# The first layer's shared expert: the last 64 of its 704 rows as one step for two token groups

## Chip, cores and metric

The kernel runs on one core of a Trainium2 chip. The metric is the device time of one execution in microseconds (us). PE is TensorE, DVE is VectorE, ACT is ScalarE, POOL is GpSimd, SP is SyncE, which issues DMAs.

## The reference, cut to what matters

Two layers, each with a state-space branch and a mixture of experts on the same layer-normed input of 2048 tokens by 256. In the first layer the experts' part has a shared expert that all tokens pass through:

```python
x = hidden_states.reshape(-1, H)                # 2048 tokens, H = 256, float32
combine = ...                                   # top 4 of 16 experts, from x @ gate_w.T
shared = _silu_mul(x @ shared_gate_up.T, SI) @ shared_down.T      # SI = 704
shared = shared * jax.nn.sigmoid(x @ shared_gate_vec.T)
# _silu_mul(gu, inter) = silu(gu[:, :inter]) * gu[:, inter:]
```

Beside it stand the routed experts (inner size 176), a selective scan over 16 states (which needs projections of x to 64 rows for delta and to 32 rows for B and C), and the second layer, which is not touched.

## The kernel before, in words

Each engine has one instruction stream, written out by hand, and semaphores order the streams against each other. Phase 0 stands between the layer norm and the first layer's loop over routed experts and scan. It does the whole shared expert, and lays the router's work and the scan's projections between its steps.

The tokens are in four groups c of 512 (NB = 4). The 704 inner rows are in six tiles f (F0 = 6): five of 128 rows and one of 64, padded with zero columns to 128. A **step** n = 6c + f, one of 24, is the "up" of one tile for one group:

- PE (`shared_up_tensor`, L699): for gate and up weights, two matmuls each over the contraction of 256, into two of the banks 0 to 3, by turns of n. It waits on `sh_free` until DVE has done step n - 2. Every float32 matmul stands as two records in the trace, so a step has 8.
- ACT (`shared_tanh`, L720): tanh of the gate's bank.
- DVE (`shared_silu`, L727 and L729): two passes that end in the slot n % 8 of the hidden activations `shT0`, which lie in the memory of the tile `y`.

When the six tiles of a group are there, the **downs** come (`shared_down_tensor`, L711): for each of the group's four blocks j of 128 tokens, six matmuls (12 records) accumulate over f into bank 4 or 5, by turns, and DVE adds the bank to x (`shared_add`, L741). A down waits on `sh_pfree` until the add two before it is done. `downs_at(n)` puts the downs of group c behind step 6c + 7, that is 7, 13 and 19; those of group 3 stand at the end of the phase, between DVE's work on delta (L961, L963).

Between the steps, by tables of the step's number:

- `SIDE_UP` and `SIDE_DOWN` place 16 **side products**. 0 to 3 are the 64-row projections (L807), 4 to 7 those for B and C (L812), 8 to 15 the products for delta (L817, contraction of 64). All use bank 7 and wait on `side_free` until the one before it has been read. For 8 to 15, ACT takes Abs and Exp (L828, L830) and DVE four passes (L853, L854, L856, L859), of which the first frees the bank and the last counts `z_free`. ACT's Ln at the end (L910) waits for all eight.
- The router: DVE builds the token lists at steps 0 to 13 (the long ones: L409 to L435 at step 7, L441 at steps 8 to 10, L449 at 11 and 12, L458 at 13), PE's 64 small matmuls that need them (L312, `route_tokens_tensor`) stand behind step 14, and DVE's last part behind step 15.

In `pads0_vector` DVE sets the padding of the weights to zero.

## Time and profile before

| | us |
|---|---|
| median of 3 runs | 1198.66 |
| lowest and highest of them | 1188.22, 1200.18 |
| the profiled execution | 1190.8 |
| its span, from the first to the last instruction | 1189.0 |
| its mean granted TensorE clock | 0.945 of full speed |

The profile is of one execution, so durations and waits are read from it and compared with its own 1190.8 us; the median of the runs is 7.9 us above it. In a timeline row the first number is the start from the span's start and the second the length in us; "[5.63 <-DVE x L741]" is the idle time of the engine before the row, and what ended it. A line such as L711 is one of the kernel before.

### The profile page before, as it was taken

What the parts mean: (1) busy time and instruction counts of PE and PEld (TensorE: products, weight loads), DVE (VectorE), ACT (ScalarE), POOL (GpSimd) and SP (SyncE); (2) the same over time, 40 slices, a digit from 0 to 9 for tenths busy, and PEclk for the clock granted to TensorE, in tenths of its full rate; (3) what the DMA queues carried; (4) which work ended last, traced back from release to release, by engine and by line L of the source; (5) the groups of instructions that cost most, each with busy time, mean ns of one, the idle gap of its engine ahead of it and who ended that gap; (6) DMA issues with size and microseconds to landing.
All of it is one profiled execution on the core that took longest, in us unless ns stands there. A gap on an engine that the chain in (4) does not pass through costs nothing.

```text
span 1189.0 us, 18608 instructions
## 1 busy us (share of the span) xinstructions
PE 970.0 (82%) x6048; PEld 573.3 (48%) x6048; DVE 902.7 (76%) x1508; ACT 495.4 (42%) x1130; POOL 413.9 (35%) x331
## 2 busy tenths in 40 slices
PE   3988998777787787774598867889988989899895
PEld 2354554444444444441545533545555655456553
DVE  4669567999999999999557644776677767777686
ACT  2201135555555555553032134544545554454542
POOL 2000010688877877763200011222322232132310
PEclk9989899999999999996899878989998999899997
DMA  6960081688878888888840042333433343244524
GB/s 217 371 187 1 12 207 47 146 155 159 161 144 163 157 157 160 139 162 169 205 140 5 1 108 54 90 95 87 112 90 94 89 109 93 68 101 101 115 43 142
DMA packets 108657, 144.30 MB, mean 121 GB/s; under 512 B 30789, under 2 KB 98899, under 8 KB 104275
## 3 DMA queue, kind: packets, MB, share of 16 engines
q0 software_dynamic: 30368, 77.92, 33.1%
q1 hardware_dynamic: 78195, 65.18, 19.8%
q8 instruction: 52, 0.85, 0.3%
q14 instruction: 42, 0.34, 0.1%
HBM read 73.72 MB, written 39.58 MB: 95 GB/s over the span
## 4 chain that ended last, share of the span: by engine, by line
PE 45%; DVE 22%; DMA 10%; issue 8%; ACT 6%; POOL 6%; SPq 2%; ACTq 1%; DVEq 0%; POOLq 0%
PE bank L699 7%; DMA sum<-yo,to_i 6%; PE bank L1902 6%; PE bank L1446 4%; PE bank L711 4%; POOL sum L1178 3%; PE bank L1452 3%; POOL xg L1185 3%; DVE cv L2159 2%; PE bank L1941 2%; PE bank L1024 2%; DVE xnT L1159 2%; PE bank L1885 2%; PE bank L1041 2%; PE bank L1894 2%
## 5 line engine op out<-in xcount | busy, mean ns | idle before, releaser
L1517 POOL DMA_INDIRECT sum<-yo,to_i x48 | 78.0, 1625 | 320.3 <-ACT yo L1475 297.9
L1185 POOL DMA_INDIRECT xg<-xn_d,token_i x80 | 95.9, 1198 | 175.7 <-DVE to_i L473 94.0
L1178 POOL DMA_INDIRECT sum<-yo,to_i x80 | 139.8, 1748 | 46.0 <-issue 21.3
L1024 PE MATMUL bank<-areaA,xgT 128*128 x320 | 116.2, 486 | 15.6 <-issue 8.7
L1041 PE MATMUL bank<-areaA,hidT 88*128 x320 | 90.7, 406 | 46.8 <-ACT hidT L1089 43.3
L2104 DVE TENSOR_TENSOR areaD<-areaD,gb 128x512 f32<-128x512 f32 x128 | 87.4, 688 | 50.6 <-ACT areaD L2051 49.6
L1902 PE MATMUL bank<-xnT,w_in 128*128 128x512 f32 x160 | 86.7, 668 | 6.6 <-ACT cv L2017 5.4
L1041 PEld LDWEIGHTS bank<-areaA,hidT 88*128 88x128 f32 x320 | 54.9, 190 | 76.4 <-issue 72.1
L1507 POOL DMA_INDIRECT xg<-xn_d,token_i x48 | 54.4, 1133 | 104.4 <-DVE to_i L473 90.0
L699 PE MATMUL bank<-xnT,areaB 128*128 128x512 f32 x192 | 86.8, 599 | 0.8 <-DVE y L729 0.8
L1024 PEld LDWEIGHTS bank<-areaA,xgT 128*128 128x128 f32 x320 | 55.0, 191 | 59.4 <-issue 42.7
L2051 ACT ACTIVATE areaD<-bank 128x512 f32<-128x512 f32 x128 | 75.8, 592 | 16.1 <-PE bank L1894 14.7
L1446 PE MATMUL bank<-wst,xgT 128*128 128x352 f32 x192 | 72.3, 501 | 5.9 <-ACT xgT L1462 3.5
L1071 ACT ACTIVATE areaB<-delta,a_neg 128x1022 f32<-128x1022 f32 x64 | 72.8, 1137 | 4.2 <-DVE areaB L1159 4.2
L2159 DVE SCALAR_TENSOR_TENSOR cv<-xpad,conv_w,cv 128x512 f32<-128x512 f32 x72 | 54.0, 750 | 15.1 <-ACT cv L2017 13.4
L720 ACT ACTIVATE areaB<-bank 128x512 f32<-128x512 f32 x24 | 14.3, 597 | 122.6 <-PE bank L699 122.6
L1096 ACT ACTIVATE yo<-bank,slot_w 128x256 f32<-128x256 f32 x80 | 37.6, 471 | 57.8 <-PE bank L1041 57.0
L994 PE MATMUL bank<-parts,pick 96*128 96x512 bf16 x128 | 40.6, 400 | 22.4 <-DVE xnT L1159 11.0
L699 PEld LDWEIGHTS bank<-xnT,areaB 128*128 128x128 f32 x192 | 35.4, 190 | 48.4 <-issue 44.4
L1941 PE MATMUL bank<-areaD,xq 128*32 128x64 f32 x2048 | 56.1, 230 | 2.9 <-DVE areaD L2112 2.9
L711 PE MATMUL bank<-areaB,y 128*128 128x256 f32 x192 | 48.8, 416 | 11.2 <-DVE x L741 11.2
L1941 PEld LDWEIGHTS bank<-areaD,xq 128*32 128x32 f32 x2048 | 35.6, 112 | 44.9 <-issue 35.2
(340 smaller groups left out, 2104.9 us busy)
## 6 DMA issues: line engine op xcount, KB each, us to landing
y<-xnT POOLq DMA_DIRECT2D x21, 1024.0 KB
wst<-gu_f SPq DMA_DIRECT2D x96, 176.0 KB
y<-areaB POOLq DMA_DIRECT2D x11, 1024.0 KB
wst<-down_f SPq DMA_DIRECT2D x48, 176.0 KB
areaA<-in_gu SPq DMA_DIRECT2D x2, 2816.0 KB
gu_f<-in_gu POOLq DMA_DIRECT2D x1, 5632.0 KB, 18.5
sum<-yo SPq DMA_DIRECT2D x2, 2176.0 KB, 16.1
down_f<-in_down POOLq DMA_DIRECT2D x1, 2816.0 KB, 24.5
```

Of the source, the lines that this page charges most:

```text
L699: last = nc.tensor.matmul(bank[:, b, :], w[:, k, f * P:(f + 1) * P], xnT[:, k, c * 512:(c + 1) * 512], start=(k == 0), stop=(k == KD - 1))
L711: last = nc.tensor.matmul(bank[:, 4 + n % 2, 0:D], shT[:, (c * F + f) % shT.shape[1], j * P:(j + 1) * P], sd[:, f, :], start=(f == 0), sto ...
L1024: last = nc.tensor.matmul(bank[:, GB + q % 2, 0:2 * FI], xgT[:, q % 2, k, :], wgu0_of(e, k), start=(k == 0), stop=(k == KD - 1))
L1041: last = nc.tensor.matmul(bank[:, HY, 0:D], hidT[:, q % 2, h, :], wd0_of(e, h), start=(h == 0), stop=(h == 1))
L1178: nc.gpsimd.indirect_dma_start(sum0_d[q % 2], bass.IndirectOffsetOnAxis(ap=to_i[:, q:q + 1], axis=0), yo[:, q % 5, :], None, compute_op=AL ...
L1185: nc.gpsimd.indirect_dma_start(xg[:, q % 5, :], None, xn_d[0], bass.IndirectOffsetOnAxis(ap=token_i[:, q:q + 1], axis=0)).then_inc(s.gathe ...
L1446: last = nc.tensor.matmul(bank[:, eb, 0:2 * FI], xgT[:, q % 2, k, :], wgu_of(q, k), start=(k == 0), stop=(k == KD - 1))
L1517: nc.gpsimd.indirect_dma_start(sum1_d, bass.IndirectOffsetOnAxis(ap=to_i[:, q:q + 1], axis=0), yo[:, q % 4, :], None, compute_op=ALU.add). ...
L1902: last = nc.tensor.matmul(o, w_in[:, k, col:col + P], xnT[:, k, b * L:(b + 1) * L], start=(k == 0), stop=(k == KD - 1))
L1941: last = nc.tensor.matmul(bank[32 * c:32 * c + 32, YB, at_t:at_t + Q], window, mm[:, g, j * Q:(j + 1) * Q], start=(old % 2 == 0 and g == 0 ...
L2104: nc.vector.tensor_tensor(mm[:, g, :].rearrange("p (j t) -> p j t", t=Q), ex[:, g % 2, :].rearrange("p (j t) -> p j t", t=Q), gb[:, step % ...
L2159: last = nc.vector.scalar_tensor_tensor(cv[:, m % 2, :], xpad[:, m % 2, i:i + L], conv_w[:, j, i:i + 1], cv[:, m % 2, :], ALU.mult, ALU.add)
```

## The change

The steps become 22. For each pair of groups (0 and 1, then 2 and 3) the 64 rows of tile 5 come first, as one step for both groups: the first group's result goes to rows 0 to 63 of the bank, the second's to rows 64 to 127, each by matmuls of 64 weight columns. Then come the five full tiles of the first group and those of the second. The table `UP_ROWS` lists the steps and `UP_SLOT` the slot of `shT0` that each writes. In a down the last matmul contracts over 64 rows only, rows 0 to 63 or 64 to 127 of the shared slot, and the 64 weight rows of `sd0` are loaded twice, once for either half. The zero padding goes.

The tables of side products and the router's step numbers are the same, so they now meet other steps: a group's last up is step 5, 10, 16 and 21, and its downs stand behind steps 7, 12 and 18 and at the end.

```diff
+        UP_ROWS = [(c, f) for p in range(NB // 2) for c, f in
+                   [(2 * p, F0 - 1)] + [(2 * p + h, f) for h in range(2) for f in range(F0 - 1)]]
+        UP_SLOT = (7, 0, 1, 2, 3, 4, 5, 6, 0, 1, 2, 3, 4, 5, 6, 0, 1, 2, 7, 4, 5, 6)
+        HALF = SI0 - (F0 - 1) * P
+        AT_UP = {row: n for n, row in enumerate(UP_ROWS)}
+        def last_up(c):
+            return AT_UP[c, F0 - 2]
+        def up0_tensor(pe, n):
+            c, f = UP_ROWS[n]
+            pe.wait_ge(s.sh_free, n + 1)
+            g = 2 * (n % 2)
+            for w, b in ((sg0, g), (su0, g + 1)):
+                for k in range(KD):
+                    if f < F0 - 1:
+                        last = nc.tensor.matmul(bank[:, b, :], w[:, k, f * P:(f + 1) * P], xnT[:, k, c * 512:(c + 1) * 512],
+                                                start=(k == 0), stop=(k == KD - 1))
+                    else:
+                        for h in range(2):
+                            last = nc.tensor.matmul(bank[h * HALF:(h + 1) * HALF, b, :], w[:, k, f * P:f * P + HALF],
+                                                    xnT[:, k, (c + h) * 512:(c + h + 1) * 512], start=(k == 0), stop=(k == KD - 1))
+            last.then_inc(s.sh_in, 1)
+        def down0_tensor(pe, c, j):
+            if j == 0:
+                pe.wait_ge(s.sh_free, last_up(c) + 1 + 2)
+            n = c * 4 + j
+            pe.wait_ge(s.sh_pfree, n + 1)
+            for f in range(F0 - 1):
+                nc.tensor.matmul(bank[:, 4 + n % 2, 0:D], shT0[:, UP_SLOT[AT_UP[c, f]], j * P:(j + 1) * P], sd0[:, f, :],
+                                 start=(f == 0), stop=False)
+            r = slice(c % 2 * HALF, (c % 2 + 1) * HALF)
+            nc.tensor.matmul(bank[:, 4 + n % 2, 0:D], shT0[r, UP_SLOT[AT_UP[c - c % 2, F0 - 1]], j * P:(j + 1) * P], sd0[r, F0 - 1, :],
+                             start=False, stop=True).then_inc(s.sh_out, 1)
...
-        UPS = NB * F0
+        UPS = len(UP_ROWS)
...
-            return (n - F0 - 1) // F0 if n > F0 and (n - 1) % F0 == 0 else None
+            return {last_up(c) + 2: c for c in range(NB - 1)}.get(n)
...
-            sp.dma_start(sd0[0:SI0 - full * P, full, :], a["sdown0"][full * P:, :]).then_inc(s.w_shared, 16)
+            for h in range(2):
+                sp.dma_start(sd0[h * HALF:(h + 1) * HALF, full, :], a["sdown0"][full * P:, :]).then_inc(s.w_shared, 16)
...
-            vec.done(nc.vector.memset(sg0[:, :, SI0:], 0.0))
-            vec.done(nc.vector.memset(su0[:, :, SI0:], 0.0))
-            rest = SI0 % P
-            last = nc.vector.memset(sd0[rest:P, F0 - 1, :], 0.0)
-            last.then_inc(s.pads, 1)
```

On PE, from the downs of group 0 to those of group 1, before (L699 an up, L711 the downs, 24 matmuls for four blocks):

```order
18 L699 MATMUL bank<-xnT,areaB 128x512 x8
19 L711 MATMUL bank<-areaB,y 128x256 x24
20 L699 MATMUL bank<-xnT,areaB 128x512 x24
21 L711 MATMUL bank<-areaB,y 128x256 x24
22 L699 MATMUL bank<-xnT,areaB 128x512 x4
23 L812 MATMUL bank<-xnT,wbc 96x512 x2
24 L312 MATMUL bank<-areaA 128x82 x64
```

Now, from the end of group 0's downs (L812 an up of a full tile, L816 the two 64-column tiles, L827 and L830 the downs, L861 the side product of L812 before):

```order
+L812 MATMUL bank<-xnT,areaB 128x512 x12
+L816 MATMUL bank<-xnT,areaB 64x512 x8
+L812 MATMUL bank<-xnT,areaB 128x512 x4
+L827 MATMUL bank<-areaB,y 128x256 x5
+L830 MATMUL bank<-areaB,y 128x256
+L827 MATMUL bank<-areaB,y 128x256 x5
+L830 MATMUL bank<-areaB,y 128x256
+L827 MATMUL bank<-areaB,y 128x256 x5
+L830 MATMUL bank<-areaB,y 128x256
+L827 MATMUL bank<-areaB,y 128x256 x5
+L830 MATMUL bank<-areaB,y 128x256
+L812 MATMUL bank<-xnT,areaB 128x512 x8
```

Six ups stood between the two groups' downs; now there are five steps, and the two ups that follow the downs of group 1 are steps 13 and 14, where one, step 14, followed before.

On PE, from the side products behind step 18 to the end of phase 0, before (L817 a side product for delta, L994 the products for the scan's first rows):

```order
32 L817 MATMUL bank<-dx,wdt 128x512
33 L699 MATMUL bank<-xnT,areaB 128x512 x4
34 L817 MATMUL bank<-dx,wdt 128x512
35 L711 MATMUL bank<-areaB,y 128x256 x6
36 L817 MATMUL bank<-dx,wdt 128x512
37 L711 MATMUL bank<-areaB,y 128x256 x6
38 L817 MATMUL bank<-dx,wdt 128x512
39 L711 MATMUL bank<-areaB,y 128x256 x12
40 L699 MATMUL bank<-xnT,areaB 128x512 x4
41 L817 MATMUL bank<-dx,wdt 128x512
42 L699 MATMUL bank<-xnT,areaB 128x512 x4
43 L817 MATMUL bank<-dx,wdt 128x512
```

and now (L866 is that side product, L1043 the scan's):

```order
48 L866 MATMUL bank<-dx,wdt 128x512 x2
49 L827 MATMUL bank<-areaB,y 128x256 x5
50 L830 MATMUL bank<-areaB,y 128x256
...
57 L827 MATMUL bank<-areaB,y 128x256 x5
58 L830 MATMUL bank<-areaB,y 128x256
59 L812 MATMUL bank<-xnT,areaB 128x512 x8
60 L866 MATMUL bank<-dx,wdt 128x512
61 L812 MATMUL bank<-xnT,areaB 128x512 x4
62 L866 MATMUL bank<-dx,wdt 128x512
63 L1043 MATMUL bank<-parts,pick 128x512 x4
```

Side products 10 and 11 stand directly behind each other, where step 19 was between them, and no up follows side product 15, where steps 22 and 23 did.

## Rows read from the trace of the kernel before

**Rows 1.** Busy times by stretch: phase 0 and the loop over experts.

```profile
core 0: us, PE busy (x) PEld busy (x) DVE busy (x) ACT busy (x) POOL busy (x), PEclk, DMA share, GB/s
0.00:204.00 204.00, 168.70 (x558) 92.36 (x558) 135.63 (x271) 44.60 (x67) 13.36 (x35) 0.97 0.49 145
204.00:600.00 396.00, 291.88 (x1202) 178.76 (x1203) 360.45 (x415) 191.89 (x474) 268.10 (x200) 0.95 0.81 160
```

**Rows 2.** Groups by line: tanh (L720) and the second pass of silu (L729).

```profile
L720 ACT ACTIVATE areaB<-bank x24: 597/597/597, 31.5 to 189.1; 128x512 f32<-128x512 f32 x24
...
L729 DVE SCALAR_TENSOR_TENSOR y<-areaB,bank x24: 686/686/689, 32.9 to 190.5; 128x512 f32<-128x512 f32 x24
```

**Rows 3.** Timeline of PE (start, length in us): downs of group 0, steps 8 to 11.

```profile
79.28 8.22 PE L711 MATMUL bank<-areaB,y 128*128 128x256 f32 x24 [5.63 <-DVE x L741]
87.34 13.90 PE L699 MATMUL bank<-xnT,areaB 128*128 128x512 f32 x32
```

**Rows 4.** Timeline of PE at the router’s four 32-column tiles and the first up.

```profile
25.91 1.92 PE L288 MATMUL bank<-xnT,wr 128*32 128x512 f32 x16 [0.84 <-ACT xnT L219]
27.77 3.70 PE L699 MATMUL bank<-xnT,areaB 128*128 128x512 f32 x8
```

**Rows 5.** Weight loads of the 64-column side product, min/median/max in ns.

```profile
L807 PEld LDWEIGHTS bank<-xnT,wdr x16: 132/136/137, 31.8 to 49.2; 128*64 128x64 f32 x16
```

**Rows 6.** Timeline of PE around the side products on 64 rows and the downs of group 2.

```profile
153.99 1.12 PE L817 MATMUL bank<-dx,wdt 64*128 64x512 f32 x2
...
159.73 2.86 PE L711 MATMUL bank<-areaB,y 128*128 128x256 f32 x12
162.51 1.12 PE L817 MATMUL bank<-dx,wdt 64*128 64x512 f32 x2
163.57 2.86 PE L711 MATMUL bank<-areaB,y 128*128 128x256 f32 x12
```

**Rows 7.** Timeline of DVE around the downs of group 1.

```profile
109.74 2.88 DVE L449 TENSOR_TENSOR areaA<-areaA,iota 128x2624 f16<-128x2624 f32 x1
...
113.86 5.62 DVE L458 TENSOR_TENSOR areaA<-areaA,token_id 128x5248 f16<-128x5248 f16 x1
119.63 0.88 DVE L741 SCALAR_TENSOR_TENSOR x<-bank,sgate,x 128x256 f32<-128x256 f32 x2 [0.16 <-DVE areaA L458]
```

**Rows 8.** Timeline of PE around the downs of group 1.

```profile
120.17 8.25 PE L711 MATMUL bank<-areaB,y 128*128 128x256 f32 x24 [5.54 <-DVE x L741]
128.26 3.60 PE L699 MATMUL bank<-xnT,areaB 128*128 128x512 f32 x8
...
133.41 2.62 PE L312 MATMUL bank<-areaA 128*128 128x82 f16 x64
```

**Rows 9.** Busy times and granted clock (PEclk) of the stretch of PE’s slow downs.

```profile
120.20:128.20 8.00, 8.00 (x24) 6.58 (x25) 0.79 (x2) 0.00 (x0) 0.00 (x0) 0.64 0.00 1
```

**Rows 10.** Timeline of PE at the end of phase 0.

```profile
180.90 1.12 PE L817 MATMUL bank<-dx,wdt 64*128 64x512 f32 x2
181.95 7.13 PE L699 MATMUL bank<-xnT,areaB 128*128 128x512 f32 x16
...
191.66 10.53 PE L711 MATMUL bank<-areaB,y 128*128 128x256 f32 x48
```

**Rows 11.** Timeline of DVE: a side product’s first step, its last, and the end of phase 0.

```profile
156.53 0.75 DVE L853 TENSOR_SCALAR delta<-bank,b_dt 128x512 f32<-128x512 f32 x1 [0.40 <-ACT dx L830]
...
185.29 0.69 DVE L859 TENSOR_TENSOR delta<-delta,yo 128x512 f32<-128x512 f32 x1
...
192.19 1.22 DVE L961 TENSOR_TENSOR delta<-delta,dx 128x1024 f32<-128x1024 f32 x1 [1.01 <-ACT dx L910]
...
202.94 0.48 DVE L741 SCALAR_TENSOR_TENSOR x<-bank,sgate,x 128x256 f32<-128x256 f32 x1
```

**Rows 12.** Timeline of ACT: the table load and Ln.

```profile
189.74 1.28 ACT L910 ACT_TABLE_LOAD   x1
191.03 3.90 ACT L910 ACTIVATE dx<-dx 128x1024 f32<-128x1024 f32 x4
```

More of the change, by code:

```diff
@@ L791, in _program @@
         hc_ready, y_added = sem("hc_ready"), [sem(f"y_added{bp}") for bp in range(2)]
+        UP_ROWS = [(c, f) for p in range(NB // 2) for c, f in
+                   [(2 * p, F0 - 1)] + [(2 * p + h, f) for h in range(2) for f in range(F0 - 1)]]
+        UP_SLOT = (7, 0, 1, 2, 3, 4, 5, 6, 0, 1, 2, 3, 4, 5, 6, 0, 1, 2, 7, 4, 5, 6)
+        HALF = SI0 - (F0 - 1) * P
+        assert 2 * HALF == P and NB == 4 and len(UP_SLOT) == len(UP_ROWS)
+        AT_UP = {row: n for n, row in enumerate(UP_ROWS)}
@@ L793, in _program, with silu0 @@
+        def silu0(v, n):
+            g = 2 * (n % 2)
+            v.wait_ge(s.sh_tanh, n + 1)
+            vec.done(nc.vector.scalar_tensor_tensor(th0[:, n % 2, :], th0[:, n % 2, :], 1.0, bank[:, g, :], ALU.add, ALU.mult))
+            v.wait_ge(vec.sem, vec.now)
+            nc.vector.scalar_tensor_tensor(shT0[:, UP_SLOT[n], :], th0[:, n % 2, :], 0.5, bank[:, g + 1, :],
+                                           ALU.mult, ALU.mult).then_inc(s.sh_free, 1)
         SIDE_UP = {0: 0, 1: 1, 2: 2, 3: 3, 4: 4, 5: 5, 14: 6, 15: 7, 16: 8, 17: 9, 18: 10, 20: 14, 21: 15}
@@ L863, in phase0_tensor @@
             pe.wait_ge(w_scan, 16 * 7)
-            pe.wait_ge(s.w_shared, 64)
+            pe.wait_ge(s.w_shared, 80)
             pe.wait_ge(s.pads, 1)
             for n in range(UPS):
-                shared_up_tensor(pe, 0, F0, sg0, su0, n)
+                up0_tensor(pe, n)
                 if n == 0:
@@ L880, in phase0_tensor @@
                             side_tensor(pe, SIDE_DOWN[c, j])
-                        shared_down_tensor(pe, 0, F0, sd0, shT0, c, j)
+                        down0_tensor(pe, c, j)
             pe.wait_ge(s.sh_free, UPS + 1)
@@ L886, in phase0_tensor @@
             for j in range(4):
-                shared_down_tensor(pe, 0, F0, sd0, shT0, NB - 1, j)
+                down0_tensor(pe, NB - 1, j)
             pe.wait_ge(s.sh_pfree, shared_done(0))
@@ L918, in phase0_vector @@
             for n in range(UPS):
-                shared_silu(v, 0, th0, shT0, n)
+                silu0(v, n)
                 if n in SIDE_UP:
@@ L2332, in pads0_vector @@
             vec.done(nc.vector.memset(wr0[:, :, E + 1:], 0.0))
-            vec.done(nc.vector.memset(sg0[:, :, SI0:], 0.0))
-            vec.done(nc.vector.memset(su0[:, :, SI0:], 0.0))
-            rest = SI0 % P
-            last = nc.vector.memset(sd0[rest:P, F0 - 1, :], 0.0)
-            last.then_inc(s.pads, 1)
+            v.wait_ge(vec.sem, vec.now)
+            v.sem_inc(s.pads, 1)
         def load1_pool(pool):
```

## The prediction

> **What bounds the kernel now.** I read the busy times by stretch first [rows 1]. The reader is to see that phase 0 takes 204 of 1189 us and has PE busy for 168.7, DVE for 135.6 and ACT for only 44.6: PE is nearest to the bound, and no engine is it throughout. The loop over the experts behind it keeps POOL's and the DMA engines' own times. Then I read the timelines of PE, DVE and ACT over phase 0 against each other. PE runs its ups back to back: 32 records take 13.90 us, and 31 distances between starts plus the last record's 0.59 give 0.43 us for a record and 3.43 us for a step [rows 3]. It waits in two places, before the third down of group 0 (5.63 us) [rows 3] and of group 1 (5.54 us) [rows 8]. There DVE is in the router's long pieces, and only the add behind them frees a bank [rows 7]. In the second place PE's 24 records then take 8.25 us, where 48 of the same kind take 10.53 at the end [rows 10]: the granted clock of that stretch is 0.64 of full speed [rows 9], that is, half clock (1.2 GHz) for most of it, after an engine that had stood still. The first place reads the same, 8.22 us for 24 [rows 3]. What ends phase 0 is a chain on DVE: four rounds of delta, dx and add from 192.19 to 202.94, started by ACT's Ln [rows 11, 12].
>
> So two steps fewer are worth what PE, and what the start of that last chain, get from them. ACT's 0.60 and DVE's 2 x 0.69 us a step [rows 2] lie beside PE's 3.43 nearly everywhere and are not the sum.
>
> **The prices.** *A paired step* has 16 records, two column tiles at a time. The nearest row is the router's product: 16 records of 512 columns on four tiles take 1.92 us, and the next up starts 1.86 after them, where one after the other they would take 16 x 0.43 = 6.9 [rows 4]. Four at a time is full overlap, so two at a time give 8 x 0.43 = 3.43, as a full step; bounds are 3.43 and, if they take turns, 6.86 us. I take the lower, since the row is of the same type and length.
>
> *A change of the tile's shape.* A side product on 64 rows has two records of 512 columns, 0.85 us, yet the next instruction starts 163.57 - 162.51 = 1.06 behind its start [rows 6]. A down of 12 records takes 2.59 us where downs follow each other: 10.53 less the last record's own 0.38, over 47 distances, is 0.216 a record [rows 10]. A down and a side product together take 163.57 - 159.73 = 3.84 [rows 6] against 2.59 + 0.85 = 3.44, so the way into the other shape and out of it costs 0.40 us. The new downs end in just such a matmul, 64 rows of 256 columns, so each of the 16 pays 0.40, and 6.4 us of PE time come back. A paired step pays 0.40 too. Bounds: nothing, if the switch hides inside an accumulation, and some 1.2 us, three times the row, since no row shows a switch within one bank's accumulation.
>
> **The change part by part**, as the shift of PE or DVE against the trace before:
>
> 1. Step 0 as a pair: +0.4. The router's product ahead of it is in yet another shape, so there is one switch more.
> 2. Downs of group 0. The first two lie inside DVE's work. The wait for the add stays, a little shorter (some 4.8 for 5.63, as PE arrives 0.4 + 2 x 0.4 later and the add 0.4 later), and I keep the half clock behind it. The last two pay 2 x 0.4, less 0.2 because the slow stretch is entered 0.4 later. Sum +1.0.
> 3. Steps 8 to 10: DVE sets the pace, unchanged; the pair of groups 2 and 3 at step 11 costs PE 0.4, which lies in PE's own short waits there. +1.0.
> 4. Downs of group 1, now behind step 12. The add that frees a bank comes directly behind the second L449 (109.74 + 2.80 = 112.54, shifted 113.5), before L458 instead of behind it; it stood at 119.63 [rows 7]. That is 6.1 earlier. PE's wait falls to some 2 us, and I expect the full clock: 2 x 2.59 = 5.2 for 128.26 - 120.17 = 8.1, a gain of 2.9 [rows 8]. Against that stand two switches (0.8) and the up of step 13, 3.4, which now follows. Step 14 starts at 120.0 + 3.4 = 123.4 for 128.26: -6.1 - 2.9 + 0.8 + 3.4 = -4.8.
> 5. L458 (5.62) now stands behind step 13, and PE's 64 matmuls that need it come behind step 14. Step 13's end, 3.63 us behind its start, tanh and silu (2.0) and L458 (5.7) give 120.0 + 11.3 = 131.3; PE would be ready at 123.4 + 3.43 + 1.72 = 128.6. So 2.7 of the gain turn into a wait here; 131.3 for 133.41 [rows 8] is -2.1. Steps 15 to 18 keep it.
> 6. Side product 11 stands directly behind 10. Bank 7 comes free when DVE's L853 is done, 156.53 + 0.75 - 153.99 = 3.3 us behind the start of 10 [rows 6, 11]; the up of step 19 covered that, and now PE waits 3.3 - 1.06 = 2.2. Products 12 and 13 still have a down of 2.99 before them. Shift +0.1.
> 7. Downs of group 2: 4 x 0.4. Shift +1.7. Steps 19 to 21 and side product 15 keep it.
> 8. The end. Before, two ups followed side product 15, and from its start to the last chain's start went 192.19 - 180.90 = 11.3 us [rows 10, 11]. Now only its own chain is left: 185.29 + 0.69 - 180.90 = 5.1 until `z_free`, then Ln, 192.19 - 191.03 = 1.2 for its first quarter [rows 11, 12]. The table load (1.28) stands ahead of that wait in ACT's order and runs inside it. 6.3 for 11.3: -5.0. What is late next is therefore side product 15, not PE: of the 6.9 us of two ups only 5.0 arrive.
> 9. The last downs take 4 x 2.99 = 12.0 on PE. DVE's chain of 10.75 starts some 3.6 behind PE's first down, and its rounds of 2.8 leave PE behind it by under 2 us; the last switch costs are covered. If a down cost 3.5 they would no longer be.
>
> Sum: +1.7 - 5.0 = -3.3 us. What stands behind the phase begins with DVE's last add, the store of x included, and so shifts whole. The extra load of 64 rows of `sd0` is one of many that PE has waited for long before its first up at 27.77 [rows 4], and the dropped zeroing lies in DVE's wait for x at the start; both count nothing. If the load were late, it would cost step 0 its own lateness. Profiled: 1190.8 - 3.3 = 1187.5. Against the median of the runs, which are up to 12 us apart, 1198.66 - 3.3 = **1195.4 us**.
>
> **Rivals.**
>
> *A: the closing matmul of 64 rows is free in an accumulation.* The terms 0.4, 0.6, 1.6 and what of the 0.8 isn't lost in waits go: about -3.4 more, -6.7, 1192.0 us. For it: the wait of one accumulation is on the bank, not on the array. Against it: rows 6, where the same 64 rows by 128 columns cost 0.40 beside full matmuls.
>
> *B: the first wait no longer costs the clock.* 4.8 us is not much under 5.63 and 5.54, and the wait may or may not be long enough for the gate. With the full clock behind group 0's downs 2.6 us come back: -5.9, 1192.8 us. Against it: the two waits that did cost it are only 0.7 to 0.8 longer, and these rows hold none in between that didn't.
>
> *C, the slower side: the two column tiles take turns.* Then a paired step has 16 x 0.43 = 6.86 us. Step 0 pays 3.43 in full, since PE has nothing to wait for there. Step 11 pays 1.4: some 2.0 of its 3.43 go into PE's short waits on DVE at steps 11 and 12 and its wait for the add. Sum -3.3 + 4.8 = +1.5, 1200.2 us. It decides from about 1.65 us extra a pair. For it: the router's tiles are four, and fill the array; two have not been seen. Against it: rows 4.
>
> *D: only the weight loads take turns.* A load for 64 columns takes 0.136 us [rows 5]; 8 of the 16 standing open make 1.1 us for step 0, and about as much for step 11: -3.3 + 2 = -1.3, 1197.4 us. The router's rows speak against it: 16 loads and matmuls in 1.92 us leave no room for loads in turn [rows 4].
>
> The Trainium skill, TensorE: Matmul & The Clock Gate, Part 3 on row/col tiling, says that a weight load overlaps a running matmul only where the two use different row groups; the two new tiles share all rows, so by that rule the time is D's or worse. This case's trace does not agree, for the full ups too load 128 by 128 weights behind running matmuls at 0.43 us a record [rows 3], so I leave the rule at D's chance.
>
> *E: the loop over experts answers to its earlier start.* Its order is fixed, but POOL's and the queues' timing is not, and three runs of one program lie 12 us apart. That may hide or multiply 3 us either way.
>
> **How the numbers follow.** My forecast has 0.46, A 0.12, B 0.14, C 0.10, D 0.08, E or something unnamed 0.10. One per cent, 12 us, is about what a measurement of this kernel can tell from no change. None of A to D leaves it; only E does: faster by over 1% 0.05, slower 0.03, within 0.92. A and B together give -9, 1189.5; the price of 1.2 us for a closing matmul gives +1.6. With a few us for the runs' own spread the range is 1187 to 1202.
>
> **What would show it.** In the changed profile: the closing matmuls of the downs (64 rows) with 0.2 us open on either side, and the last 48 records of downs at 12.0 us; paired steps with 16 records in about 3.6; PE's wait before group 1's third down at about 2 us and no low clock there; a new wait of 2.7 on the matmuls for the token lists and one of 2.2 on the second side product of two; 6.3 us from the last side product to the last chain; phase 0 over at about 200. I'd be wrong most by a paired step of over 5 us, or by downs of over 3.4.

## The result and the profile after

| | before | after |
|---|---|---|
| median of the comparison, us | 1194.84 (20 runs) | 1199.54 (20 runs) |
| lowest, highest | 1188.22, 1200.36 | 1191.38, 1205.8 |
| ratio, 95% interval | | 1.0043 [1.0027, 1.006] |
| profiled execution, us | 1190.8 | 1198.37 |
| its span, mean granted clock | 1189.0, 0.945 | 1196.5, 0.938 |

Forecast were 3.3 us less; measured are 4.7 more. Two repeats (below) gave 1.0054 and 1.0035. The change costs time, by some 0.4%. A ratio is worked out from the single executions and not from the two medians, so the two can differ by some 0.2%; two executions of the experiments, each over 1.5% above the fastest of its kernel (the first of batch 1, the first of batch 2), are left out of it.

The windows of after come first (the columns are those of [rows 1]).

```profile
0.00:204.00 204.00, 167.60 (x559) 86.95 (x560) 132.97 (x264) 45.18 (x68) 13.94 (x36) 0.97 0.49 147
204.00:600.00 396.00, 294.04 (x1178) 177.52 (x1176) 353.91 (x394) 188.05 (x466) 270.30 (x194) 0.93 0.81 159
```

The reader is to see that phase 0 has the same granted clock as before, 0.97, although a gain of clock was forecast, and that the loop over the experts, whose code is unchanged, has less: 0.93 for 0.95 [rows 1], and PE is busy for 2.2 us more in it.

PE's timeline of after, phase 0 and the border to the loop:

```profile
28.48 3.65 PE L816 MATMUL bank<-xnT,areaB 128*64 128x512 f32 x16
32.06 0.66 PE L297 MATMUL bank<-ident,areaA 128*128 128x128 f32 x4
...
80.09 3.97 PE L827 MATMUL bank<-areaB,y 128*128 128x256 f32 x10 [5.04 <-DVE x L741]
...
84.62 2.43 PE L827 MATMUL bank<-areaB,y 128*128 128x256 f32 x10
86.97 0.70 PE L830 MATMUL bank<-areaB,y 64*128 64x256 f32 x2
87.60 10.57 PE L812 MATMUL bank<-xnT,areaB 128*128 128x512 f32 x24
...
113.45 4.11 PE L827 MATMUL bank<-areaB,y 128*128 128x256 f32 x10 [1.91 <-DVE x L741]
...
132.53 2.63 PE L312 MATMUL bank<-areaA 128*128 128x82 f16 x64 [2.58 <-DVEq L462]
...
156.46 1.12 PE L866 MATMUL bank<-dx,wdt 64*128 64x512 f32 x2 [2.23 <-DVE delta L902]
157.51 3.86 PE L827 MATMUL bank<-areaB,y 128*128 128x256 f32 x10
...
184.54 1.12 PE L866 MATMUL bank<-dx,wdt 64*128 64x512 f32 x2
...
193.75 2.42 PE L827 MATMUL bank<-areaB,y 128*128 128x256 f32 x10 [0.63 <-DVE x L741]
...
202.10 0.44 PE L1065 MATMUL bank<-ident,xg 128*128 128x128 f32 x2 [2.32 <-DVE x L741]
203.29 2.71 PE L1073 MATMUL bank<-areaA,xgT 128*128 x4 [0.75 <-ACT xgT L1128]
```

Nearly every price is as forecast. The paired step's 16 records take 3.65 us, the next instruction starts 3.58 behind it: two column tiles at a time, fully. A down takes 87.60 - 84.62 = 2.98 us, 0.39 more than before. PE's waits are 5.04 us (forecast 4.8), 1.91 (2), 2.58 for the token lists (2.7) and 2.23 for side product 11 (2.2). What is not as forecast are three rows behind waits: the ten records of L827 take 4.11 us at 113.45 and 3.86 at 157.51, where 2.43 is their time at 84.62, and the four products of the first expert take 2.71 us at 203.29. In PE's timeline of before these four take 1.45 us, behind a shorter wait:

```profile
203.47 0.44 PE L1016 MATMUL bank<-ident,xg 128*128 128x128 f32 x2 [1.29 <-DVE x L741]
204.73 1.45 PE L1024 MATMUL bank<-areaA,xgT 128*128 x4 [0.82 <-ACT xgT L1079]
```

The windows of after's three stretches (columns as above, the granted clock third from the end) say why:

```profile
113.45:117.50 4.05, 4.05 (x11) 2.85 (x11) 0.34 (x1) 0.00 (x0) 0.00 (x0) 0.58 0.00 0
157.50:161.40 3.90, 3.90 (x12) 2.69 (x11) 3.02 (x5) 1.32 (x2) 0.00 (x0) 0.61 0.80 131
203.20:206.00 2.80, 2.71 (x5) 1.61 (x6) 0.00 (x0) 1.84 (x1) 0.94 (x1) 0.50 1.09 387
```

Half clock, each time behind a wait of about 2 us. Before, PE waited 5.63 and 5.54 us and paid for each [rows 3, 8, 9].

DVE's timeline of after, then ACT's, around group 1 and at the end of the phase:

```profile
110.11 2.88 DVE L449 TENSOR_TENSOR areaA<-areaA,iota 128x2624 f16<-128x2624 f32 x1
112.92 0.87 DVE L741 SCALAR_TENSOR_TENSOR x<-bank,sgate,x 128x256 f32<-128x256 f32 x2
...
126.79 5.62 DVE L458 TENSOR_TENSOR areaA<-areaA,token_id 128x5248 f16<-128x5248 f16 x1
...
190.81 1.23 DVE L1010 TENSOR_TENSOR delta<-delta,dx 128x1024 f32<-128x1024 f32 x1 [1.18 <-ACT dx L959]
...
201.57 0.48 DVE L741 SCALAR_TENSOR_TENSOR x<-bank,sgate,x 128x256 f32<-128x256 f32 x1
```

```profile
189.65 3.90 ACT L959 ACTIVATE dx<-dx 128x1024 f32<-128x1024 f32 x4 [1.30 <-DVE delta L908]
```

The add stands behind the second L449 and ahead of L458, as forecast, and the last side product is followed by its own chain: 190.81 - 184.54 = 6.27 us for the forecast 6.3. Phase 0's last add stands at 201.57 for 202.94 [rows 11], 1.37 earlier; since PE's first up began 0.71 later in this execution (28.48 for 27.77 [rows 4]), the phase itself is 2.1 us shorter, where 3.3 were forecast. That can't make a kernel whose span is 7.5 us longer. In these two executions the loss is behind the phase, most of it in the loop over the experts. POOL's timeline has its first and last scatter, of before:

```profile
213.71 1.65 POOL L1178 DMA_INDIRECT sum<-yo,to_i  x1 [0.30 <-issue]
...
549.30 2.59 POOL L1178 DMA_INDIRECT sum<-yo,to_i  x1 [1.14 <-ACT yo L1096]
```

and of after:

```profile
213.22 1.64 POOL L1227 DMA_INDIRECT sum<-yo,to_i  x1 [0.50 <-issue]
...
555.41 2.59 POOL L1227 DMA_INDIRECT sum<-yo,to_i  x1 [0.98 <-ACT yo L1145]
```

From first to last it is 335.6 us before and 342.2 after. Of the 1.37 us gained, 0.49 are left at the first scatter (the rest went at the border), then 6.6 are lost in the loop and 1.4 behind it.

### The profile page after: what moved, and what is told of

It reads as the page before. It is cut to its first block and busy times, and to the rows that moved or that the text cites. A ratio compares the mean times of both kernels' runs of the same rounds, so it can differ in the third digit from the quotient of the medians.

```text
span 1196.5 us, 18599 instructions
## 1 busy us (share of the span) xinstructions
PE 975.0 (81%) x6048; PEld 570.9 (48%) x6048; DVE 900.0 (75%) x1501; ACT 495.6 (41%) x1128; POOL 418.2 (35%) x331
## 5 line engine op out<-in xcount | busy, mean ns | idle before, releaser
L1566 POOL DMA_INDIRECT sum<-yo,to_i x48 | 78.3, 1632 | 320.6 <-ACT yo L1524 300.1
L1227 POOL DMA_INDIRECT sum<-yo,to_i x80 | 144.8, 1810 | 43.7 <-DMA sum<-yo,to_i 21.7
L1073 PE MATMUL bank<-areaA,xgT 128*128 x320 | 122.7, 509 | 16.2 <-issue 10.7
L1073 PEld LDWEIGHTS bank<-areaA,xgT 128*128 128x128 f32 x320 | 57.8, 200 | 61.0 <-issue 45.4
L812 PE MATMUL bank<-xnT,areaB 128*128 128x512 f32 x160 | 72.3, 600 | 0.3 <-DVE y L839 0.3
L2208 DVE SCALAR_TENSOR_TENSOR cv<-xpad,conv_w,cv 128x512 f32<-128x512 f32 x72 | 54.0, 750 | 15.5 <-ACT cv L2066 13.8
L720 ACT ACTIVATE areaB<-bank 128x512 f32<-128x512 f32 x22 | 13.1, 597 | 117.1 <-PE bank L812 108.6
L1043 PE MATMUL bank<-parts,pick 96*128 96x512 bf16 x128 | 41.4, 406 | 20.8 <-DVE xnT L1208 11.4
L1133 ACT ACTIVATE act_t<-bank 128x176 f32<-128x176 f32 x80 | 25.2, 315 | 74.3 <-PE bank L1073 73.6
L1212 DVE TENSOR_TENSOR xnT<-xnT,bank 128x1024 f32<-128x1024 f32 x42 | 51.2, 1220 | 3.7 <-DVE xnT L1208 0.5
```

What stands on the lines that cost most here:

```text
L812: last = nc.tensor.matmul(bank[:, b, :], w[:, k, f * P:(f + 1) * P], xnT[:, k, c * 512:(c + 1) * 512], start=(k == 0), stop=(k == KD - 1))
L1073: last = nc.tensor.matmul(bank[:, GB + q % 2, 0:2 * FI], xgT[:, q % 2, k, :], wgu0_of(e, k), start=(k == 0), stop=(k == KD - 1))
L1227: nc.gpsimd.indirect_dma_start(sum0_d[q % 2], bass.IndirectOffsetOnAxis(ap=to_i[:, q:q + 1], axis=0), yo[:, q % 5, :], None, compute_op=AL ...
L1566: nc.gpsimd.indirect_dma_start(sum1_d, bass.IndirectOffsetOnAxis(ap=to_i[:, q:q + 1], axis=0), yo[:, q % 4, :], None, compute_op=ALU.add). ...
```

## The experiments

Kernels of one batch share the runs of the kernel before, so each table row is to be compared with its own batch. A **filler** is a matmul of 128 by 128 weights on 256 columns into a bank that is free at the time; nobody reads what it computes. It sits where PE would wait, and keeps it busy.

| batch | kernel | median, us (runs) | before | ratio, 95% interval |
|---|---|---|---|---|
| 1 | closing matmul of 128 rows | 1196.01 (12) | 1197.08 (35) | 0.9983 [0.9953, 1.0012] |
| 1 | before, extra load | 1195.5 (12) | | 0.9973 [0.9944, 1.0002] |
| 1 | before, two steps left out | 1191.94 (12) | | 0.9951 [0.9927, 0.9976] |
| 1 | after, fillers at the border | 1196.69 (12) | | 1.001 [0.9983, 1.0037] |
| 2 | after again | 1203.69 (12) | 1195.11 (29) | 1.0054 [1.0025, 1.0084] |
| 2 | after, all waits filled | 1186.53 (6) | | 0.9915 [0.9882, 0.9949] |
| 2 | before, its two long waits filled | 1190.8 (11) | | 0.9963 [0.9936, 0.9989] |
| 2 | closing 128 rows, all waits filled | 1188.22 (12) | | 0.9919 [0.9892, 0.9945] |
| 3 | after, all filled but the border | 1190.72 (12) | 1196.63 (29) | 0.9932 [0.9905, 0.996] |
| 3 | after, all waits filled, again | 1190.08 (12) | | 0.9946 [0.992, 0.9972] |
| 3 | after, reordered, no fillers | 1192.8 (12) | | 0.997 [0.9943, 0.9997] |
| 3 | all together | 1181.77 (6) | | 0.9886 [0.9845, 0.9927] |
| 4 | after again | 1199.56 (12) | 1195.77 (35) | 1.0035 [1.0005, 1.0065] |
| 4 | after, fillers at the border | 1196.81 (12) | | 1.0017 [0.9988, 1.0046] |
| 4 | after, all filled but the border | 1191.61 (12) | | 0.9969 [0.9942, 0.9996] |
| 4 | after, group 1's wait filled | 1200.94 (12) | | 1.0034 [1.0005, 1.0062] |

### 1. The closing matmul over all 128 rows

The second copy of the 64 weight rows goes to memory of its own, and the other half of each copy is zero. (`UP_SLOT[...]` is shortened here.)

```diff
-            r = slice(c % 2 * HALF, (c % 2 + 1) * HALF)
-            nc.tensor.matmul(bank[:, 4 + n % 2, 0:D], shT0[r, UP_SLOT[...], j * P:(j + 1) * P], sd0[r, F0 - 1, :],
+            w5 = sd0b[:, :] if c % 2 else sd0[:, F0 - 1, :]
+            nc.tensor.matmul(bank[:, 4 + n % 2, 0:D], shT0[:, UP_SLOT[...], j * P:(j + 1) * P], w5,
```

> The changed kernel, but the closing matmul of each down contracts over all 128 rows, with a second copy of the 64 weight rows and zeros in the other half, so that no down changes the tile's shape. Theory S (the 64-row matmuls are what costs): phase 0 ends some 3 us earlier than in the changed kernel, and the total falls by 3 to 5 us, to the time of before or below it (ratio to before 0.998 to 1.001). Theory L (the loop over experts is slower after the change, for a reason at its border that isn't in the downs): phase 0 ends 3 us earlier, but the total keeps most of its loss, ratio to before 1.002 to 1.005.

Measured: 0.9983 [0.9953, 1.0012]. PE's timeline of it:

```profile
112.55 3.44 PE L828 MATMUL bank<-areaB,y 128*128 128x256 f32 x10 [2.49 <-DVE x L741]
...
130.84 4.12 PE L312 MATMUL bank<-areaA 128*128 128x82 f16 x64 [2.58 <-DVEq L462]
...
186.26 2.32 PE L828 MATMUL bank<-areaB,y 128*128 128x256 f32 x10
188.42 0.59 PE L831 MATMUL bank<-hid,y 128*128 128x256 f32 x2
188.85 2.32 PE L828 MATMUL bank<-areaB,y 128*128 128x256 f32 x10
```

A down is back at 188.85 - 186.26 = 2.59 us, so the 0.39 are the price of the 64-row shape, and rival A, that it is free in an accumulation, is wrong. The new thing to see is row 130.84: the token lists' matmuls, 2.63 us in after, take 4.12 here, behind the same wait of 2.58 us. The slow stretch behind short waits is there again, at another wait too; group 1's ten records take 3.44 us for 2.32. The ratio is what the first theory expected, that the 64-row matmuls are what costs, although phase 0's last add stands at 200.65, only 0.9 us earlier than in after, and not 3. What this run says of the cause is weighed below.

### 2. Before, with the extra load

```diff
-            sp.dma_start(sd0[0:SI0 - full * P, full, :], a["sdown0"][full * P:, :]).then_inc(s.w_shared, 16)
+            for h in range(2):
+                sp.dma_start(sd0[h * 64:(h + 1) * 64, full, :], a["sdown0"][full * P:, :]).then_inc(s.w_shared, 16)
```

> The kernel before with only the loads and the padding of the change: the 64 rows of the down weights are loaded twice (rows 64 to 127 are multiplied by zeros), and the zeroing of these rows is gone. Theory D (the extra transfer shifts the queues and with them the loop): ratio to before 1.003 to 1.005. Theories S and L: 1.000, within 0.001.

Measured: 0.9973 [0.9944, 1.0002]. The load and the zeroing that is dropped with it cost nothing that shows, as the prediction took it.

### 3. Before, without the last two steps

Steps 22 and 23 are left out, so the last group's last two tiles are not computed, and its downs read stale slots.

```diff
-            pe.wait_ge(s.sh_free, c * F + F + 2)
+            pe.wait_ge(s.sh_free, c * F + F + 2 - (2 if l == 0 and c == NB - 1 else 0))
...
-        UPS = NB * F0
+        UPS = NB * F0 - 2
```

> The kernel before without its steps 22 and 23 (the last two tiles of group 3 are left out; the downs of group 3 then read old slots, so their values are not the reference's). Phase 0 ends some 5 us earlier, since side product 15 is then last, and PE still runs full-shape downs. If the loop over experts keeps its length whenever it starts, the total falls by 5 us, ratio to before 0.996. Theory L (a border at which side product 15's chain ends phase 0 harms the loop): the total falls by 1 or not at all, ratio 0.999 to 1.003.

Measured: 0.9951 [0.9927, 0.9976], 5.1 us off the median. The prediction's step 8 gives these two steps 5.0, and phase 0's last add stands at 197.98 for 202.94. Time that the end of phase 0 gains thus does reach the end of the kernel. PE waits 2.72 us at this border, longer than after does, and yet the first expert's four products take 1.45 us, full clock. An excess behind the phase is not the loop's answer to an earlier start as such, which rival E held.

### 4. After, with a warm border

```diff
+            for i in range(5):
+                nc.tensor.matmul(bank[:, 7, 0:D], sd0[:, 0, 0:P], sd0[:, 0, :], start=True, stop=True)
```

behind the last down, in the wait of 2.32 us at 202.10.

> The changed kernel with five extra matmuls of 128x256 on PE behind the last down, into bank 7, which nobody reads, in place of PE's wait of 2.3 us for DVE's last add. Theory C (PE stands still at the border, the clock falls, and the loop starts late on PE and keeps it): no half clock at the start of the loop and 1 to 5 us less than the changed kernel, ratio to before 1.000 to 1.003. If the border's clock costs nothing that lasts: as the changed kernel, 1.004.

Measured: 1.001 [0.9983, 1.0037]. PE's timeline of it:

```profile
113.76 2.43 PE L827 MATMUL bank<-areaB,y 128*128 128x256 f32 x10 [1.91 <-DVE x L741]
...
131.15 3.59 PE L312 MATMUL bank<-areaA 128*128 128x82 f16 x64 [2.58 <-DVEq L462]
134.54 4.32 PE L812 MATMUL bank<-xnT,areaB 128*128 128x512 f32 x8
...
156.66 2.07 PE L866 MATMUL bank<-dx,wdt 64*128 64x512 f32 x2 [2.22 <-DVE delta L902]
158.66 4.63 PE L827 MATMUL bank<-areaB,y 128*128 128x256 f32 x10
...
205.00 1.45 PE L1075 MATMUL bank<-areaA,xgT 128*128 x4 [0.75 <-ACT xgT L1130]
```

The products at the border take 1.45 us for 2.71. And here group 1's wait, the same 1.91 us, costs nothing, while those for the lists and for side product 11 do. A wait of 2 us may or may not be followed by the half clock.

### 5. The waits filled: after, before, and with the full rows

The changed kernel gets fillers before the third down of group 0 and of group 1, before the token lists, before side product 11 and at the border. The kernel before gets 12 in each of its two long waits. The kernel with full rows gets 12, 5, 6, 4 and 6 in the five places. The lines for the changed kernel:

```diff
+        def fill_tensor(pe, count, b, free, at):
+            pe.wait_ge(free, at)
+            for i in range(count):
+                nc.tensor.matmul(bank[:, b, 0:D], sd0[:, 0, 0:P], sd0[:, 0, :], start=True, stop=True)
...
+                    fill_tensor(pe, 5, 2, s.sh_free, 16)
...
+                                fill_tensor(pe, 4, 6, s.indices, 1)
...
+                            fill_tensor(pe, (11, 4, 0)[c], 7, side_free, 6)
...
+            fill_tensor(pe, 5, 7, side_free, 16)
```

> The changed kernel once more, on the same chip as the next three, and with a second profile. All theories: ratio to before 1.002 to 1.006. Theory C (the clock falls at the new short waits): low clock behind at least one of the waits for the add of group 1, for the token lists and for side product 11; the length of phase 0, from the first up to the last delta, differs between profiles by 1 to 4 us (before had 172.8, the changed kernel 170.7).

> The changed kernel with filler matmuls of 128x256 in PE's waits of phase 0, whose results nobody reads: 11 before the third down of group 0, 4 before that of group 1, 5 before the token lists, 4 before side product 11 and 5 at the border to the loop. Theory C (what the change loses is the clock behind waits of 2 us, of which there are four now and none before): no low clock from the first up to the loop, phase 0 some 167 us for 170.7, total 3 to 5 us under the changed kernel. If the clock is not it: the total of the changed kernel.

> The kernel before with 12 such filler matmuls before the third downs of groups 0 and 1, its two long waits. Theory C: phase 0 some 167 to 168 us for 172.8, total 5 us less, ratio to before 0.994 to 0.997. This is the same phase 0 length that theory C gives the changed kernel with fillers: with the clock out of the way the change gains nothing, since six shape changes on the path take what the two steps give.

> The changed kernel with closing matmuls over 128 rows (no change of shape in the downs) and fillers in the waits (12, 5, 6, 4 and 6). Theories C and S together: phase 0 some 164 us, 3 less than either kernel with fillers, ratio to before 0.991 to 0.995. If the shape changes cost nothing on the path: as the changed kernel with fillers.

Measured: 1.0054, 0.9915, 0.9963 and 0.9919 (intervals above). The changed kernel and its filled version, the same useful work, lie 17 us apart in the medians of this batch; the filled one has only 6 runs, and in batch 4 it is 8.0 us, with the border left as it is. The kernel before gains 4.3. With the waits filled, full rows give nothing that shows (0.9919 for 0.9915). PE's timeline of the kernel before, filled, shows the fillers (L867) and the downs at full clock, 5.45 us for 8.22 [rows 3] (the second place has 5.45 too, for 8.25 [rows 8]):

```profile
74.42 5.34 PE L867 MATMUL bank<-areaB 128*128 128x256 f32 x24
80.23 5.45 PE L711 MATMUL bank<-areaB,y 128*128 128x256 f32 x24 [0.46 <-DVE x L741]
```

### 6. Border or waits, and the best version

The first kernel is that of 5 without the border's line, the second that of 5 once more. The third moves side products 11 to 13 behind the next down and the router's last pieces behind the next step, so that a down stands in one short wait and an up in the other, and has no fillers; the fourth puts together that order, the full rows and fillers where waits are left.

```diff
-        SIDE_DOWN = {(2, 0): 11, (2, 1): 12, (2, 2): 13}
+        SIDE_DOWN = {(2, 1): 11, (2, 2): 12, (2, 3): 13}
-        RANKS_UP, TOKENS_UP = 5, 14
+        RANKS_UP, TOKENS_UP = 5, 15
...
-                if n == 15:
+                if n == 16:
```

> The kernel with fillers f_after, without the five fillers at the border to the loop: PE again waits 2 us and more for DVE's last add before its first work of the loop. Theory B (the fall at the border is worth more than its own matmuls, since it delays the first experts): the first scatter of the loop comes 0.8 to 3 us later behind the last delta than the 13.2 of f_after in those executions whose clock falls, and the total lies 3 to 5 us above f_after (ratio to before 0.995 to 0.997). If the border costs only its own matmuls: about 1 us above f_after (0.992 to 0.994).

> f_after once more, for its small number of runs and to compare with g1_cold_border on the same chip. Both theories: no low clock in phase 0, its length 166 us; ratio to before 0.990 to 0.995.

> The changed kernel without fillers, with two places of its tables moved: side products 11 to 13 stand behind the first, second and third down of group 2 (so a down of 3.0 us covers the bank that 11 waits for), and the matmuls for the token lists behind step 15, not 14 (DVE's last part behind 16). The waits of 2.2 and of 2.6 us go, a wait of about 2 for side product 7 comes. If what the change lost is these waits and their clock: phase 0 some 4 us shorter than the changed kernel on average (167 to 170.5), ratio to before 0.999 to 1.002. If the loss lies elsewhere: 1.004 as the changed kernel.

> All together: closing matmuls over 128 rows, side products 11 to 13 and the token lists moved as in g3_reorder, and fillers in the waits that are left (12, 6, 4 and 7). By the prices so far phase 0 is 161 to 162 us, 2 less than f_full and 11 less than before, ratio to before 0.988 to 0.992. If fillers overshoot the waits, each costs 0.43.

Measured: 0.9932, 0.9946, 0.997 and 0.9886. With phase 0's waits filled the border makes no difference that shows. The reordered kernel, which takes two of the short waits away with useful work, is at 0.997 [0.9943, 0.9997] where after is at 1.0035 to 1.0054 in other batches. In its profile a wait of 1.96 us for side product 7 is new, with no slow row behind it, and group 1's ten records still take 4.11 us. All together are **0.9886 [0.9845, 0.9927]**, 1181.77 us in 6 runs: faster than the kernel before in the same batch, and far below after's ratios. PE's timeline of the best shows the lists' matmuls without a wait, an up, fillers (L827) and a side product ahead of them:

```profile
124.81 3.60 PE L813 MATMUL bank<-xnT,areaB 128*128 128x512 f32 x8
128.24 1.89 PE L827 MATMUL bank<-areaB 128*128 128x256 f32 x8
130.35 1.96 PE L870 MATMUL bank<-xnT,wbc 128*96 128x512 f32 x4 [0.23 <-DVE yo L898]
132.15 2.63 PE L312 MATMUL bank<-areaA 128*128 128x82 f16 x64
```

### 7. Which waits: one batch for all

> The changed kernel as it is, as the base of the three others of this call. Theory P, that the half clock behind the changed kernel's waits inside phase 0 makes its time, and theory Q, that the cold TensorE at the border to the loop (the wait ahead of the scan's first products) makes it, both expect 1.004 to 1.006 of the kernel before, 4 to 7 us above it, as the first two measurements gave.

> The changed kernel with five filler matmuls in the wait at the border alone; nobody reads what they compute. Theory Q: most of the excess goes, 4 to 6 us below the changed kernel. Theory P: under 1.5 us below it, the 1.3 us by which the four products at the border get shorter.

> The changed kernel with fillers in its waits inside phase 0 (behind the second down of groups 0 and 1, for the token lists, for side product 11), none at the border. Theory P: 7 to 13 us below the changed kernel and 4 to 7 below the kernel before. Theory Q: the half clock of phase 0 alone comes back, some 5 us, and the excess of the border stays, so that it ends at the kernel before or within 2 us of it.

> The changed kernel with four fillers in one wait alone, that behind the second down of group 1. If the drop of the clock belongs to this wait, it goes and the run is 1.5 to 3 us below the changed kernel. If short waits follow each other and the next one takes the drop over (as one profile with a warm border showed it, at the waits for the token lists and for side product 11), the time stays within 1 us of the changed kernel and the profile shows as much half clock in phase 0 as before.

Their edits are the lines of 5: the border's alone (`h_border`), all but the border's (`h_waits`), and of these only group 1's, with `(0, 4, 0)[c]` (`h_group1`). Medians: 1199.56, 1196.81, 1191.61 and 1200.94. The border is worth 2.8 us, less than the runs can tell; the waits inside phase 0 are worth 8.0. Filling group 1's wait alone shows no gain (1.0034 for 1.0035), but intervals of 0.3% to either side can't tell the 1.7 us that one stretch of half clock costs. Its timeline of PE:

```profile
114.34 1.99 PE L826 MATMUL bank<-areaB 128*128 128x256 f32 x8
116.32 2.42 PE L835 MATMUL bank<-areaB,y 128*128 128x256 f32 x10
...
133.71 4.12 PE L312 MATMUL bank<-areaA 128*128 128x82 f16 x64 [2.58 <-DVEq L462]
...
160.19 3.72 PE L835 MATMUL bank<-areaB,y 128*128 128x256 f32 x10
```

The downs behind the fillers (L826) take 2.42 us for 4.11, and the token lists 4.12 for 2.63. In this profile the half clock stands at the next wait, as it did with a warm border in experiment 4. That the filling moved it there is not shown: in the repeat of after in batch 2 neither place has it, and with full rows both have. Where all four are filled none is left, as PE's timeline of that kernel shows:

```profile
79.47 2.42 PE L835 MATMUL bank<-areaB,y 128*128 128x256 f32 x10
...
111.28 2.42 PE L835 MATMUL bank<-areaB,y 128*128 128x256 f32 x10
...
128.67 2.63 PE L312 MATMUL bank<-areaA 128*128 128x82 f16 x64 [0.42 <-DVEq L462]
...
153.66 2.42 PE L835 MATMUL bank<-areaB,y 128*128 128x256 f32 x10
```

### The loop over the experts in all of them

From first to last scatter, beside the granted clock of 215 to 545 us, in all eighteen profiles:

| clock | loop, us |
|---|---|
| 0.99 | before 335.6 |
| 0.98 | before filled 336.3; before without two steps 337.4; after with a warm border 337.1 (batch 4); after filled 334.8 (batch 3); reordered 336.1; after with group 1's wait filled 338.3 |
| 0.97 | before with the extra load 338.7; full rows 339.1; after with a warm border 339.4 (batch 1); after with all but the border filled 340.3 (batch 3) and 340.5 (batch 4); after 340.6 (batch 4) |
| 0.96 | after 342.2 and 341.6; after filled 343.4 (batch 2); full rows filled 341.2; all together 337.7 |

These are the windows, of before, after and after filled (batch 2):

```profile
215.00:545.00 330.00, 257.56 (x1044) 152.24 (x1042) 313.04 (x329) 175.62 (x445) 250.50 (x179) 0.99 0.83 154
```

```profile
215.00:545.00 330.00, 261.82 (x1033) 155.03 (x1032) 307.20 (x324) 172.92 (x439) 250.44 (x177) 0.96 0.81 151
```

```profile
215.00:545.00 330.00, 258.88 (x1015) 154.04 (x1016) 305.57 (x324) 171.04 (x435) 247.26 (x175) 0.96 0.83 152
```

The order of the lengths is nearly that of the clocks, over 8.6 us (all together is the exception), and the loop's code is the same in all. All three profiles of after stand at 0.96 or 0.97, the one of before at 0.99; but one kernel, after filled, has 343.4 once and 334.8 once. So what the change does to the loop's clock is not told by one profile of each.

## Why the prediction was wrong

**The costs of the instructions held.** Step 0 as a pair is 3.65 us, so C (tiles take turns) and D (weight loads take turns) are out. The Trainium skill's rule that the prediction set beside D (TensorE: Matmul & The Clock Gate, Part 3, that a weight load overlaps a running matmul only in other row groups) is not borne out by this row: the two tiles share all rows. A down of 2.98 us against 2.59 with full rows rules out A. The Trainium skill, TensorEngine Tiling (Array Packing), Key Properties, says that a change of the tiling mode drains TensorE; this case's trace agrees in so far as the way in and out costs 0.39 us.

**The waits held too**, all four within 0.3 us, and so did the end chain of step 8 (6.27 us) and the cover of step 9, but for a wait of 0.63 us at 193.75.

**Step 4 failed**, at the words "PE's wait falls to some 2 us, and I expect the full clock", which carry -2.9 us. The sum of -3.3 was thus -0.4 of work and -2.9 of clock. **Steps 5 and 6 lacked the same term**: they put waits of 2.7 and 2.2 us where there was none and priced only the waiting.

Seven profiles have these three waits unfilled or mostly so (after three times, the full rows, the warm border twice, group 1's wait filled). Half clock came behind group 1's in four of six, behind the lists' in three of seven, behind side product 11's in all seven; it cost 1.5 to 1.8 us each time (4.11 for 2.43, 4.12 for 2.63, 3.86 for 2.43 and the closing 0.91 for 0.70), and once 3.2 (side product 11 in experiment 4). That is two drops in an execution in the mean, where the prediction has none at these three. Before, two long waits had one each.

B, that the first wait keeps the clock, is wrong too: ten records of 3.93 to 4.64 us for 2.43 or 2.32 behind a wait of 5.04 to 5.64. Step 2 kept that drop at some 2.7 us, and it varied: 1.5 to 2.8 us in five profiles, 4.6 in two, where the next ten records are slow as well (4.30 and 4.33). In the three profiles of after the half clock of phase 0 thus took 4.9, 4.4 and 7.9 us, as much in the mean as the 5.8 of before. The gain of 2.9 didn't come. Phase 0's last add stands at 201.57, 200.61 and 204.46 there, 0.7 us before the 202.94 of before in the mean, and from PE's first up on the phase is 1.2 us shorter and not 3.3.

**The sum's last words failed too**, that what stands behind the phase begins with DVE's last add "and so shifts whole". From that add to the first scatter of the loop go 10.8 us in before, and 11.7, 13.9 and 13.8 in the three profiles of after. The two of after with only the border filled have 10.8 again.

**Is the clock the cause?** Filling the waits inside phase 0 took the changed kernel from 1199.56 to 1191.61 in one batch, from above the kernel before, 1.0035 [1.0005, 1.0065], to below it, 0.9969 [0.9942, 0.9996]; so that filling these waits takes away more than the whole excess is shown. The same treatment took 4.3 us off the kernel before. With the clock held in both, the change is worth -0.5% to +0.1%: 0.9932 and 0.9969 for the changed kernel (two measurements, the border unfilled), 0.9915 and 0.9946 (border filled), 0.9963 for the kernel before; only 0.9915 is of its batch. The profiles tell it more finely: from PE's first up to phase 0's last add it is 169.6 us in the kernel before, filled, and 168.2 in all four profiles of the changed one, filled. So the work was worth -1.4 us in phase 0, where the prediction's sum has -0.4. The extra load and an answer of the loop to an earlier start are excluded by experiments 2 and 3.

The single executions point to the clock as well. The mean granted clock is 0.942 in the 128 executions of the kernel before that the four batches hold, and 0.935 in the 43 of the changed kernel that its three ratios rest on. Within either kernel 0.01 less goes with some 7.5 us more, so 0.007 less would be some 5 us, about the excess. That is a correlation, and it doesn't say where in the kernel the clock was lower.

One result doesn't fit so simply. The full rows alone (experiment 1) are at 0.9983 [0.9953, 1.0012], with three stretches of half clock behind short waits in their profile, and yet below after's three ratios. With the waits filled they gave nothing that shows, though phase 0's last add came 2.9 us earlier (193.10 for 195.99). So how much of the excess is the clock's and how much the changes of shape make is not settled by the medians.

**What stays open** is how the excess behind phase 0 comes about. The profiles of after have the first scatter at 213.22, 214.55 and 218.25 for 213.71, then 5.0 to 6.6 us more in the loop, at a lower clock; but the one profile of before is of a short execution, 1190.8 us for a median of 1194.84, and the three kernels made from it by small edits have 336.3 to 338.7 us in the loop, so part of these 5.0 to 6.6 is the execution's and not the kernel's. The border is a place that no step of the prediction looked at: PE's wait ahead of the first expert grew to 2.32 us, with half clock behind it, from 1.29 in the profile of before. All eight profiles with a grown wait and a slow row there have 11.5 to 13.9 us from the last add to the first scatter; of the ten others eight have 10.8 and two, both filled, 12.2 and 12.5. Filling the border gave 2.8 us in the medians, from 1.0035 to 1.0017 with overlapping intervals, and nothing that shows where phase 0 was filled (0.9932 against 0.9946). So PE's state at the border costs up to 3 us by the first scatter; that it bears on the loop's clock too is argued and not shown. The 8.0 us of the fillers inside phase 0 need no further way: its last add comes 6.1 us earlier with them (196.07 in the mean of four profiles for 202.21 in the mean of three), and the runs can't tell 6.1 from 8.0.

The range, 1187 to 1202, holds 1199.5, and the change is within 1%. The direction is wrong. Of the rivals only C had a time above before, for a reason that isn't there, and E left the direction open. Missing was the rival "short waits cost the clock as long ones do". Its price stood in the rows: -3.3 + 2.9 for step 4, some 1.5 for each of the two new waits and for the border, half of the 2.9 of [rows 8], makes up to +4, an estimate from [rows 8].

## What to carry to other kernels

A wait of TensorE costs its length and perhaps a stretch at half clock behind it, a short one too. So list PE's waits of the whole phase as they will be, the border to the next phase among them, and price each new one at both clocks: a change that shortens two waits but makes new short ones can lose. Closing one of several waits was no test here, since one drop is smaller than the runs can tell and the next wait may have it; close all, with an order in which useful work stands in them or, where that can't be, with matmuls that nobody reads.

## What the runs showed of the hardware

- Half clock came behind a wait of 1.91 us (ten records in 4.11 us) and in another execution of the same program did not (2.43). Two kernels differ at the border as well: 2.32 us with half clock behind it (2.71 for 1.45), 2.72 without (1.45).
- Two column tiles of 64 with float32 weights ran fully side by side: 16 records of 512 columns in 3.65 us, as 8 of full width in 3.70.
- A matmul of 64 rows that closes an accumulation of 128-row ones made it 0.39 us longer (2.98 for 2.59).
